# Decoder layer: GpSimd's normalization and rotations cut into steps and placed later, the second router transpose moved

## What is computed

```python
def _layernorm(x, eps=1e-05):
    m = jnp.mean(x, axis=-1, keepdims=True)
    v = jnp.var(x, axis=-1, keepdims=True)
    return (x - m) / jnp.sqrt(v + eps)

def _apply_rope(x, cos, sin):
    rot = jnp.stack((-x[..., 1::2], x[..., 0::2]), axis=-1).reshape(x.shape)
    return x * cos + rot * sin

# self attention, 16 heads of 16
q = concat([q_c, _apply_rope(q_e, cos, sin)]); k = concat([k_c, _apply_rope(k_e, cos, sin)])
scores = where(causal, q @ k.T / 4, -inf)
x = x + (softmax(scores) @ v) @ Wc
# cross attention, keys and values from ctx_1024
x = x + xattn(_layernorm(x), ctx_1024)
# experts: each takes its 512 best tokens by the router's scores
logits = _layernorm(x) @ router_w + router_b
x = x + experts(_layernorm(x), softmax(logits))
```

## Time and profile before

| | |
|---|---|
| three runs | 1289.25, 1292.88, 1294.58 us (median 1292.88) |
| the profiled execution | 1295.45 us |
| its span, first to last instruction | 1293.7 us |
| mean granted clock of TensorE | 0.939 of full speed |
| busy: TensorE, VectorE, ScalarE, GpSimd | 1144.6, 969.7, 713.2, 530.1 us |

### The profile page before, as it was taken

One profiled execution on the slowest core, in us unless ns is written; L12 is line 12 of the kernel. 1 busy time (PEld: TensorE's weight loads), 2 busy tenths in 40 slices (PEclk: granted clock), 3 DMA queues, 4 the chain that ended last, 5 costly groups with the idle time before them and its releaser, 6 DMA issues. The chain is left out here.

```text
span 1293.7 us, 21922 instructions
## 1 busy us (share of the span) xinstructions
PE 1144.6 (88%) x7616; PEld 683.2 (53%) x7616; DVE 969.7 (75%) x2633; ACT 713.2 (55%) x1429; POOL 530.1 (41%) x728
## 2 busy tenths in 40 slices
PE   5699999999999999999999999999996218999994
PEld 2454545555455554544445454545333217888984
DVE  6678788788888778888888887878861577666551
ACT  6035555545555556676767676666773104565561
POOL 4656375654758443434242424240212003454332
PEclk9669899899999999999999999999999558999997
DMA  5551533515335243342525252415110504454322
GB/s 169 114 116 33 117 85 80 115 35 131 84 99 126 91 115 98 102 100 81 116 66 116 66 115 67 99 54 112 34 42 25 185 4 164 111 112 119 98 26 25
DMA packets 89330, 117.94 MB, mean 91 GB/s; under 512 B 12065, under 2 KB 59105, under 8 KB 89090
## 3 DMA queue, kind: packets, MB, share of 16 engines
q1 hardware_dynamic: 83074, 107.97, 32.5%
q0 software_dynamic: 6144, 8.52, 4.0%
HBM read 48.63 MB, written 16.91 MB: 51 GB/s over the span
## 5 line engine op out<-in xcount | busy, mean ns | idle before, releaser
L785 ACT ACTIVATE probs<-ps_st 128x512 f32<-128x512 f32 (+3 forms) x1024 | 476.5, 518 | 269.6 <-PE ps_st L618 265.6
L638 PE MATMUL ps_p<-kst,qst 63*128 63x512 f32 (+3 forms) x1024 | 383.5, 436 | 9.7 <-DVE mx L895 8.0
L618 PE MATMUL ps_st<-qst,kst 64*128 64x512 f32 (+3 forms) x1024 | 360.1, 419 | 9.2 <-ACT probs L785 8.4
L893 DVE TENSOR_REDUCE mx<-ps_p 128x1 f32<-128x512 f32 x512 | 322.3, 681 | 43.0 <-PE ps_p L638 42.2
L618 PEld LDWEIGHTS ps_st<-qst,kst 64*128 64x128 f32 x1024 | 165.9, 187 | 261.7 <-ACT probs L785 199.9
L895 DVE CUSTOM_DVE_ANT_0 ps_p<-ps_p,tri 128x128 f32<-128x128 f32 (+3 forms) x512 | 238.1, 515 | 13.7 <-PE ps_p L638 12.6
L599 PE MATMUL ps_o<-probs,vals 128*32 128x512 f32 (+3 forms) x2048 | 234.4, 530 | 14.6 <-POOL probs L508 14.6
L638 PEld LDWEIGHTS ps_p<-kst,qst 63*128 63x128 f32 x1024 | 172.5, 189 | 35.3 <-DVE mx L895 15.8
L450 POOL TENSOR_SCALAR lnw<-mv 128x4 f32<-128x4 f32 x24 | 5.1, 211 | 337.1 <-DVE mv L879 337.0
L508 POOL TENSOR_SCALAR_AFFINE_SELECT probs<-probs 128x512 f32<-128x512 f32 x128 | 79.2, 635 | 85.9 <-ACT probs L785 85.5
L1278 PE MATMUL moe_ps_y<-moe_w,moe_hid_h 128*128 128x256 f32 x512 | 94.6, 283 | 0.0
(11 more groups left out here) (224 smaller groups left out, 1893.5 us busy)
## 6 DMA issues: line engine op xcount, KB each, us to landing
qst<-qk_h SPq DMA_DIRECT2D x64, 256.0 KB, 4.7
kst<-qk_h SPq DMA_DIRECT2D x64, 256.0 KB, 4.9
qst<-qk_l SPq DMA_DIRECT2D x32, 256.0 KB, 5.4
kst<-qk_l SPq DMA_DIRECT2D x32, 256.0 KB, 4.9
moe_w1r<-in_w_dram SPq DMA_DIRECT2D x8, 1024.0 KB, 5.0
moe_w2r<-in_w_dram SPq DMA_DIRECT2D x8, 1024.0 KB, 9.9
xin<-in_x_dram SPq DMA_DIRECT2D x8, 512.0 KB, 4.1
xres<-in_x_dram SPq DMA_DIRECT2D x8, 512.0 KB, 3.9
```

What stands on the lines that cost most here:

```text
L618: last = nc.tensor.matmul(out, kst[rows, t % 2, pair, kt * P:(kt + 1) * P], qst[rows, t % 2, pair, lo:S], start=True, stop=not masked)
L638: last = nc.tensor.matmul(ps_p1[:, i % 3, 0:keys], qst[rows, t % 2, pair, qt * P:(qt + 1) * P], kst[rows, t % 2, pair, 0:keys], start=True ...
L785: nc.scalar.activation(probs[:, kt, j, 0:n], ps_st[:, i % 2, 0:n], ACT.Exp, scale=float(DH) ** -0.5).then_inc(exp_done, 1)
L893: nc.vector.tensor_reduce(mx[:, g % 2, at:at + 1], bank, AX.X, ALU.max).then_inc(max_done, 1)
```

## The change

`ln` stays as VectorE's step. GpSimd's part of it becomes two steps of its own: `norm` at far + 13 waits for the statistics and computes r (`deviation`), and `scale` at far + 15 makes (x - mean) r with the two operands `mean` and r in one instruction a tile (`normalize`); the two operations for m are gone. For `ln3` both follow one another in one step. The pooled part of `qk` becomes `rotate` two places behind the product and `split_qk` four places behind it; the wait for the last turn's stacking now stands ahead of the split. For turn 1 `norm` and `scale` stand where `ln` does. The second `xt3` goes from after + 47 to after + 51.

```diff
--- before.py
+++ after.py
@@ -94,10 +94,15 @@
         put(far - SPAN + 14, "xload", t)
 
         put(far - 4 if t == 1 else far + 10, "ln", t)
+        put(far - 4 if t == 1 else far + 13, "norm", t)
+        put(far - 4 if t == 1 else far + 15, "scale", t)
         put(far + (17 if t == 1 else 23), "xt", t, 0)
         put(far + (18 if t == 1 else 27), "xt", t, 1)
         for i in range(4):
-            put(far + ((19, 36, 43, 50) if t == 1 else (35, 43, 51, 59))[i], "qk", t, i // 2, i % 2)
+            at_qk = far + ((19, 36, 43, 50) if t == 1 else (35, 43, 51, 59))[i]
+            put(at_qk, "qk", t, i // 2, i % 2)
+            put(at_qk + 2, "rotate", t, i // 2, i % 2)
+            put(at_qk + 4, "split_qk", t, i // 2, i % 2)
             put(far + (65, 66, 75, 76)[i], "stack", t, i // 2, i % 2)
         put(near + 11, "v", t, 0)
         put(near + 15, "v", t, 1)
@@ -114,7 +119,7 @@
             put(after + 33, "ln3", t)
             put(after + 45, "table", t)
             put(after + 47, "xt3", t, 0)
-            put(after + 47, "xt3", t, 1)
+            put(after + 51, "xt3", t, 1)
             put(after + 55, "lg", t, 0)
             put(after + 67, "lg", t, 1)
 
@@ -445,19 +450,19 @@
                 ins.then_inc(pool_chain, 1)
                 pool.wait_ge(pool_chain, chain[0])
 
-            def layernorm(x, i, done):
-                v, y, a, m = (lnw[:, i, k, :] for k in range(4))
+            def deviation(i):
+                v, y, a = (lnw[:, i, k, :] for k in range(3))
                 link(nc.gpsimd.tensor_scalar(out=v, in0=mv[:, i, :, 1], scalar1=1.0, scalar2=EPS, op0=ALU.mult, op1=ALU.add))
                 link(nc.gpsimd.tensor_tensor(out=y, in0=v, in1=half_neg[:, :], op=ALU.pow))
                 link(nc.gpsimd.tensor_tensor(out=a, in0=y, in1=y, op=ALU.mult))
                 link(nc.gpsimd.tensor_tensor(out=a, in0=a, in1=v, op=ALU.mult))
                 link(nc.gpsimd.tensor_scalar(out=a, in0=a, scalar1=-0.5, scalar2=1.5, op0=ALU.mult, op1=ALU.add))
                 link(nc.gpsimd.tensor_tensor(out=y, in0=y, in1=a, op=ALU.mult))
-                link(nc.gpsimd.tensor_tensor(out=m, in0=mv[:, i, :, 0], in1=y, op=ALU.mult))
-                link(nc.gpsimd.tensor_scalar(out=m, in0=m, scalar1=-1.0, scalar2=0.0, op0=ALU.mult, op1=ALU.add))
+
+            def normalize(x, i, done):
                 for t in range(TT):
-                    last = nc.gpsimd.tensor_scalar(out=xn[:, t, :], in0=x[:, t, :], scalar1=y[:, t:t + 1],
-                                                   scalar2=m[:, t:t + 1], op0=ALU.mult, op1=ALU.add)
+                    last = nc.gpsimd.tensor_scalar(out=xn[:, t, :], in0=x[:, t, :], scalar1=mv[:, i, t, 0:1],
+                                                   scalar2=lnw[:, i, 1, t:t + 1], op0=ALU.subtract, op1=ALU.mult)
                 last.then_inc(done, 1)
 
             def split(hi, lo, src, done):
@@ -467,15 +472,17 @@
             def run(steps):
                 for s in steps:
                     kind = s[0]
-                    if kind == "ln":
+                    if kind == "norm":
+                        pool.wait_ge(stats_ready, s[1] + 1)
+                        deviation(0)
+                    elif kind == "scale":
                         t = s[1]
-                        pool.wait_ge(stats_ready, t + 1)
                         if t > 0:
                             pool.wait_ge(m_ready, M[("xt", t - 1, 1)] + 1)
                         if t - 4 >= B:
                             pool.wait_ge(m_ready, M[("xt3", t - 4, 1)] + 1)
                             pool.wait_ge(rows_stored, 16 * (t - 4 - B + 1))
-                        layernorm(xin, 0, xn_ready)
+                        normalize(xin, 0, xn_ready)
                     elif kind == "ln3":
                         t = s[1]
                         pool.wait_ge(stats3_ready, t - B + 1)
@@ -484,22 +491,24 @@
                         if t > B:
                             pool.wait_ge(m_ready, M[("xt3", t - 1, 1)] + 1)
                             pool.wait_ge(rows_stored, 16 * (t - B))
-                        layernorm(xres, 1, xn3_ready)
-                    elif pooled(s):
+                        deviation(1)
+                        normalize(xres, 1, xn3_ready)
+                    elif kind == "rotate" and pooled(("qk",) + s[1:]):
+                        s = ("qk",) + s[1:]
                         t, side, r = s[1:]
                         if is_cross(t):
                             pool.wait_ge(h_done, HI[s] + 1)
+                            link(nc.gpsimd.tensor_tensor(out=rope[:, r, :], in0=rope[:, r, :], in1=some_key[:, :], op=ALU.mult))
                         else:
                             evicted(pool, s)
-                        if t > 0:
-                            pool.wait_ge(stacked, 16 * STACK_DMAS * t)
-                        src = rope[:, r, :]
-                        if not is_cross(t):
                             src, turn = (rope_of(s)[:, i, :] for i in range(2))
                             link(nc.gpsimd.tensor_tensor(out=turn, in0=turn, in1=sinb, op=ALU.mult))
                             link(nc.gpsimd.tensor_tensor(out=src, in0=src, in1=turn, op=ALU.add))
-                        else:
-                            link(nc.gpsimd.tensor_tensor(out=src, in0=src, in1=some_key[:, :], op=ALU.mult))
+                    elif kind == "split_qk" and pooled(("qk",) + s[1:]):
+                        t, side, r = s[1:]
+                        if t > 0:
+                            pool.wait_ge(stacked, 16 * STACK_DMAS * t)
+                        src = rope[:, r, :] if is_cross(t) else rope_of(("qk",) + s[1:])[:, 0, :]
                         split(qk_h[:, side, r, :], qk_l[:, side, r, :], src, q_pool)
                     elif kind == "tri":
                         g, kt = s[1:]
@@ -537,7 +546,7 @@
                             last = nc.gpsimd.tensor_tensor(out=xres[:, tt, :], in0=xres[:, tt, :], in1=bo[:, :], op=ALU.add)
                         last.then_inc(res_bias, 1)
 
-            first = STEPS.index(("ln", 0)) + 1
+            first = STEPS.index(("scale", 0)) + 1
             run(STEPS[:first])
             nc.gpsimd.memset(vals[:, :, :, :].rearrange("p a b c -> p (a b c)"), 1.0).then_inc(pool_prep, 1)
             pool.wait_ge(rope_loaded, 16)
```

## The result

The changed kernel takes 1285.01 us (median of 13 runs, 1282.92 to 1287.37) where the kernel before takes 1291.58 us (13 runs, 1288.27 to 1294.62): the ratio is 0.9946, with a 95% interval of 0.9934 to 0.9957. That is 6.6 us less, some 0.5%. The forecast was 11.7 us less (1281.2 us), so the direction was right, the time lies in the range (1273 to 1290), and the gain is a little over half of the one forecast. The profiled execution took 1285.01 us.

What follows compares the result with a forecast made beforehand. TensorE, busy 88%, was taken to set the pace, so only its waits count. Maskings 6.0, router transposes 4.6 and normalization 1.1 summed to 11.7 us off the 1292.88 us median: 1281.2 us, range 1273 to 1290.

Steps and rivals of the forecast that it cites:

- The maskings: Self attention: moved rotation and split end TensorE's waits for GpSimd's maskings; 0.95 us a turn, 6.0 us in all.
- the first wait: Self turn, TensorE's values product of place 46, 0.86 us late for a masking; 0.2 us of it counted as gain.
- the third: Self turn, third stall for a masking, 0.62 us; no rotation written just before it, so 0.6 us counted as gain.
- some 13: Sign in self attention: TensorE's wait for VectorE's maxima rises from 5.7 to some 13 us.
- VectorE's wait for the split: Sign in self turns: VectorE's wait for the rope split rises above 1.17 us at the third rotation too.
- The clock: TensorE's clock falls in two self turns, costing 5.2 us; the sum takes them as they are, counting no gain.
- rival 1: Three masking stalls count in full and slow clock stretches go too: 1273 us, with the clock 1268; chance 0.15.
- The router's second half: Cross turns: second transpose xt3 at 51 no longer waits for VectorE; six stalls of 0.77 us, 4.6 us off.
- The row operation: GpSimd's normalization: new form stays at 558 ns; dropping two small operations saves 0.56 us in two places, 1.1 us.
- The sum: Whole kernel: maskings 6.0, transposes 4.6 and normalization 1.1 make 11.7 us off, forecast 1281.2 us.
- Rival 2: Self turns: the maskings' stalls turn wholly into waits for VectorE's maxima, turn stays at 53.1 us; 1287 us, chance 0.15.
- Rivals 3 and 4: 3: moved transpose's gain is given back, 1286 us, chance 0.15. 4: maskings delay rotations, 1305 us, chance 0.07.

Runs made afterwards that it cites:

- e2: Changed kernel with the four tiles of a normalization in four forms (subtract-mult, add-mult, mult-add, mult-subtract): 1285.88 us, single run.
- e7: Changed kernel with the old row operation, a second rope buffer, and the split two places later, so a masking comes between rotation and split: 1268.08 us, single run.
- e12: The same kernel as e7, run again four times: 1272.88 us.

## Why the prediction was right or wrong

**The maskings.** Right in the main: all 20 waits went, no rotation was delayed. GpSimd in the changed kernel, masking 37 ahead of the rotation, as the earlier trace rows have it behind:

```profile
156.78 0.63 POOL L517 TENSOR_SCALAR_AFFINE_SELECT probs<-probs 128x512 f32<-128x512 f32 x1 [4.39 <-ACT probs L794]
158.89 1.28 POOL L505 TENSOR_TENSOR rope<-rope,late 128x512 f32<-128x512 f32 x1 [1.48 <-DVE rope L941]
...
162.33 1.29 POOL L470 TENSOR_TENSOR qk_l<-rope,qk_h 128x512 fp32r<-128x512 f32 x1
163.57 1.23 POOL L517 TENSOR_SCALAR_AFFINE_SELECT probs<-probs 128x512 f32<-128x512 f32 x2
```

What was behind the wait was named, and its share was mis-sized. TensorE in the same turn, and VectorE's writing of `rope` with the read-out of the maximum that TensorE waits for:

```profile
165.37 0.44 PE L647 MATMUL ps_p<-kst,qst 63*128 63x384 f32 x1 [0.61 <-DVE mx L904]
...
178.02 0.44 PE L647 MATMUL ps_p<-kst,qst 63*128 63x384 f32 x1 [0.60 <-DVE mx L904]
...
189.67 0.43 PE L647 MATMUL ps_p<-kst,qst 63*128 63x384 f32 x1 [0.36 <-DVE mx L904]
```

```profile
163.72 0.69 DVE L940 TENSOR_TENSOR rope<-ps_m,late 128x512 f32<-128x512 f32 x1 [1.17 <-POOL qk_l L470]
...
165.17 0.14 DVE L904 DVE_READ_ACCUMULATOR2_ANT mx<- 128x1 f32 x1
```

VectorE starts 1.17 us late as before, and the score product starts at 165.37, 1.65 us behind it; before, by the middle of a merged row, it was about 1.8. I counted 0.2 us for the first wait, 0.35 for the first two. But VectorE's own rhythm didn't change: from its first late writing of `rope` to its second it takes 176.37 - 163.72 = 12.65 us now and took 288.81 - 276.13 = 12.68 before. What TensorE gained there it waited for the maxima again; together the two brought under 0.1 us. For the third I wrote that it has "no rotation written just before it" and counted 0.6. VectorE from its `ot` copy to its statistics, before and then in the changed kernel:

```profile
295.09 0.69 DVE L906 TENSOR_TENSOR ot_l<-ps_m,ot_h 128x512 fp32r<-128x512 f32 x1 [0.64 <-ACT ot_h L799]
...
299.52 1.39 DVE L876 BATCH_NORM_STATS2 stats<-xin 128x6 f32<-128x256 f32 x4
```

```profile
182.63 0.69 DVE L915 TENSOR_TENSOR ot_l<-ps_m,ot_h 128x512 fp32r<-128x512 f32 x1 [0.64 <-ACT ot_h L808]
...
186.69 1.39 DVE L885 BATCH_NORM_STATS2 stats<-xin 128x6 f32<-128x256 f32 x4
```

It took 4.43 us and takes 4.06, so 0.37 us remain of the 0.62. From 182.63 on VectorE now has no idle time until behind the third wait shown (189.67, 0.36 us): it is full there, and this is what limits the third gain. Together 0.43 us a turn against 0.95: 2.6 us of 5.7. The wait for maxima rose to 16.9 us, where "some 13" was said. VectorE's wait for the split did not appear at the third rotation, whose input (170.10) still waits for TensorE's product; it stays at 14.4 us in 12 places.

**The clock.** The forecast took it "as it is". In the profiled executions the two long turns, 5.2 us, were gone. But the changed kernel lost 1.1 us more than the kernel before from 467 to 585 us (118.56 us for 117.44), with clock falls to 0.79 and 0.82 in it where the kernel before has one to 0.79, and 0.7 us more at the end of the cross turns, beyond its longer wait for `xn`, at a clock of 0.79 and 0.54 from 976 to 992 us. The medians hold less still: the two profiled executions of the kernel before had 2 and 1 falls in these turns. So the part of rival 1 that spoke of the clock came true in the self turns and only in part over the whole; a term for it belonged into the sum, of 1.4 us by what is left over below (an estimate, and not measured by itself). The Trainium skill's rule ("TensorE: Matmul & The Clock Gate", "What's actually happening"), that activity releases the clock, agrees with 0 falls in 48 self turns against 10 in 36. The falls from 460 to 500 us, which are no rarer without the waits for maskings, it does not tell apart.

**The router's second half.** Right in mechanism, too small in size: 1.07 us a turn in place of 0.77, and 6.8 us in all in place of 4.6.

**The row operation.** This step failed. I took the present 558 ns "since these are one kind of instruction of one shape", and widened it by 10%. It took 1220 ns. The bound rested on kind and shape; the pair of operations was new to the trace, and its rows with a subtraction, of two tiles, showed it as fast as an addition (1292 ns). No row could have shown a factor of 2.2, so the upper end should have been a multiple and not 10%. The two places on the path went from a gain of 1.1 us to a loss of 4.2, which is 5.3 us and the largest miss. e2 shows the cause down to the operation, `subtract`.

**The sum.** 2.6 + 6.8 - 4.2 = 5.2 us of steady parts, 6.6 measured; the 1.4 between them is what falls of the clock can account for, though the runs don't resolve it part by part. Against the forecast of 11.7 us the row operation missed by 5.3 and the maskings by 3.4 one way, the transposes by 2.2 and the clock by about 1.4 the other. That the time lies well inside the range is in part luck: with the first two misses alone the forecast's sum gives 3.0 us off and 1289.9 us, next to the range's end at 1290.

**The rivals.** Rival 2 was in the main true of the maskings: 14.6 us of their waits went, and the wait for maxima rose by 11.2. Rivals 3 and 4 fell: the move of `xt3` gave nothing back, and no rotation waited for exponentials. That no masking stands between the steps was right, and e7 and e12 show that nothing is lost by it.

## What to carry to other kernels

When a wait goes, look for the ring behind it, and change both: here either alone brought 0.4 us a turn and both 1.84, and the kernel with a second `rope` buffer and the old row operation takes 1271 us, 22 us less than the kernel before beside it. An operation that the trace doesn't show gets a bound of a multiple, or is measured, even where its shape and its kind are known. And a change of several parts can hide one that should be left out: without the new row operation the changed kernel is 5.7 us faster (e1).

## What the runs showed of the hardware

On GpSimd a two-step operation (`tensor_scalar`, fp32) with two column operands takes 558 to 565 ns for 128x256 as mult-add or add-mult, and 1220 to 1234 ns when one of the two is `subtract`, first or second (e2). The same engine's `tensor_tensor` of 128x512 takes 1292 ns as `subtract` and as `add`. TensorE's granted clock fell in self turns only in kernels in which TensorE waited for the maskings (0.2 to 1.6 us each), 10 times in 36 turns, at a cost of 0.2 to 2.8 us each; in other stretches it fell in both kinds of kernel, and the cause of a fall stays open.
